# A two-layer decoder on one core: from a front half and a back half with their own buffers to two streams that each carry every other batch

## The chip, the cores and the metric

One Trainium2 chip, one core. The metric is the device time of one execution in microseconds (us). Four batches of 512 tokens by 256 channels pass through the decoder; nothing is sent to another core.

## The reference, cut to what matters

Each batch goes through six blocks, each of them "x = layernorm(x + block(x))":

```python
x = _layernorm(x + _L0_attn_ref(x, ...))                      # causal softmax attention, one head of 256
x = _layernorm(x + _L0_xattn_ref(x, ctx, ctx, mask, ...))     # masked cross attention, then its own layernorm
x = _layernorm(x + _L0_ffn_ref(x, k0, k1, k2, ...))           # +1/-1 weights, 512 -> 1024 -> 1024 -> 256
x = _layernorm(x + _L1_attn_ref(x, ...))                      # 16 heads, relu features, running sums
x = _layernorm(x + _L1_xattn_ref(x, ctx, ctx, ...))           # mLSTM: 8 heads, gates, decay matrix
x = _layernorm(x + _L1_ffn_ref(x, w1, conv_w, conv_b, w2))    # rounded linear, 3-tap convolution, silu, rounded linear
```

## The kernel before

The batch is cut into a **front half** (self attention "self", cross attention "cross", signed layers "sign", relu attention "perf") and a **back half** ("mlstm" and the rounded network "quant"). Tokens are in four tiles of 128. Each half has a set of buffers of its own (activations x and y, turned activations xT and ctxT, a work region, small columns) and four of the eight PSUM banks, which it uses in rotation. `front_half(b)` works in set 0 and `back_half(b)` in set 1, so the front of batch b+1 runs beside the back of batch b. That gives five stages: the front of batch 0 alone (stage 0), three stages with a front and a back side by side (stages 1 to 3), and the back of batch 3 alone (stage 4).

Each of the halves is a generator for each engine, which yields the name of a step before it issues the step's instructions. `weave` (L344) merges the generators of an engine: it always takes the step with the lowest due time. The due times are the tables `FRONT_TIMES` and `BACK_TIMES` (L40, L169), one column for each engine, plus 189 for each batch; the back of batch b starts with the front of b+1. The order so found is the order of the instructions in the queue of the engine, and each engine works its queue strictly from the front. Stage 0 also carries "prep" steps (`PREP_TIMES`, L293): ScalarE (ACT) makes the signed weights (`prep.w1*`, `prep.w2`, L2057 and L2060) and sums absolute values (`prep.abs*`, L2068), VectorE (DVE) rounds the weights of the last network (`prep.round*`, L1515 to L1520).

The lines that matter below:

- L824 `keep_clock(u, n)`: n matmuls of 512 bf16 columns (L827) into a bank that is free, whose result nobody reads. It stands ahead of the last product of the self attention of batch 0 (8) and of its `sign.xT0` (7), in every front half ahead of `perf.ft` (2, twice), `perf.state` (3, twice), `perf.fq.1` and `perf.fk.1` (3 each), in every back half ahead of `mlstm.cols` (3, in the last 6), and in the last back half ahead of `mlstm.xT0` (8), `quant.turn0` (8), `quant.row1` (6) and `quant.topT` (8). That makes 115.
- `perf` on TensorE (PE): feature products L1063 and L1077, states L1097, scores L1115. `mlstm.cols` begins at L1258; `mlstm.head*` follow.
- `quant`: DVE writes the hidden tile (L1954) and adds two of the three taps (L1966, L1969) to the middle one, which ACT makes (L2274). In the last back half PE makes two taps with diagonal matrices (`two_taps`, L1362; the matrices are built on POOL at L2391), DVE adds the third (L1962) and ACT skips its tap.
- `quant.down`: four token tiles of eight matmuls (L1409), each matmul behind the rounding of its slice of the hidden layer. In the last back half the first three tiles are made together, slice by slice (L1399).
- `front_half` on PE waits, ahead of the first self score (L872), for ACT's copies of both q and v.
- ctxT is loaded twice a batch, once for each half.

Of the kernel before, what the change touches and what calls it, by code (L numbers as in the profile page):

```python
# [8 lines left out]
U8 = mybir.dt.uint8  # L9
# [23 lines left out]
AMONG = ("cv0", "cv1")  # L33

FRONT_TIMES = [  # L40
    ("self.q", 1, None, 1, None),
    ("self.v", 2, None, 2, None),
    ("self.score0", 3, 4, 3, None),
    ("self.cv0", 4, 5, None, None),
    ("self.score1", 5, 6, 4, None),
    ("self.cv1", 6, 7, None, None),
    ("self.score2", 7, 9, 5, None),
    ("self.product0", 8, 10, 8, None),
    ("self.score3", 9, 11, 9, None),
    ("self.stats0", None, 13, None, None),  # L50
    ("self.product1", 10, 12, 10, None),
    ("self.score4", 11, 14, 11, None),
    ("self.product2", 12, 15, 12, None),
    ("self.norm0", None, 16, 13, None),
    ("self.stats1", None, 19, None, None),
    ("self.score5", 13, 17, 14, None),
    ("self.product3", 14, 18, 15, None),
    ("cross.shift0", None, 21, None, None),
    ("cross.shift1", None, 23, None, None),
    ("self.norm1", None, 20, 17, None),  # L60
    ("cross.shift2", None, 24, None, None),
    ("cross.xT0", 16, None, 16, None),
    ("cross.shift3", None, 25, None, None),
    ("cross.fold", 15, None, 19, None),
    ("cross.bar0", None, 26, None, None),
    ("cross.bar1", None, 27, None, None),
    ("cross.bar2", None, 28, None, None),
    ("self.rstd0", None, None, None, 4),
    ("cross.q0", 19, None, 20, None),
    ("cross.bar3", None, 30, None, None),  # L70
    ("cross.xT1", 20, 31, None, None),
    ("cross.score0", 23, 33, 23, None),
    ("self.rstd1", None, None, None, 5),
    ("cross.score1", 24, 34, 24, None),
    ("cross.q1", 22, None, 22, 6),
    ("cross.score2", 25, 37, 28, None),
    ("cross.product0", 26, 41, 29, None),
    ("cross.score3", 28, 42, 30, None),
    ("cross.in_stats0", None, 44, None, None),
    ("cross.product1", 29, 43, 31, None),  # L80
    ("cross.in_norm0", None, 45, None, None),
    ("cross.score4", 30, 46, 32, None),
    ("cross.product2", 31, 47, 34, None),
    ("cross.add0", None, 49, None, None),
    ("cross.in_rstd0", None, None, None, 7),
    ("cross.stats0", None, 50, None, None),
    ("cross.score5", 32, 51, 36, None),
    ("cross.product3", 33, 52, 37, None),
    ("cross.in_stats1", None, 53, None, None),
    ("cross.in_norm1", None, 54, None, None),  # L90
    ("cross.add1", None, 56, None, None),
    ("cross.rstd0", None, None, None, 8),
    ("cross.stats1", None, 57, None, None),
    ("cross.norm0", None, 55, 39, None),
    ("cross.in_rstd1", None, None, None, 9),
    ("sign.xT0", 38, 66, 44, None),
    ("sign.early", 47, None, None, None),
    ("cross.norm1", None, 67, 49, None),
    ("sign.xT1", 48, 70, 50, None),
    ("sign.a0", 52, 76, 51, None),  # L100
    ("cross.rstd1", None, None, None, 11),
    ("sign.a1", 53, 77, 52, None),
    ("sign.a2", 57, 78, 53, None),
    ("sign.a3", 58, 79, 54, None),
    ("sign.a4", 59, 80, 56, None),
    ("sign.a5", 60, 83, 57, None),
    ("sign.a6", 61, 84, 58, None),
    ("sign.a7", 62, 85, 60, None),
    ("sign.b0", 64, 86, 61, None),
    ("sign.b1", 65, 94, 63, None),  # L110
    ("sign.b2", 66, 97, 66, None),
    ("sign.b3", 67, 98, 67, None),
    ("sign.b4", 68, 102, 68, None),
    ("sign.b5", 69, 103, 69, None),
    ("sign.b6", 70, 108, 70, None),
    ("sign.c0", 72, 110, None, None),
    ("sign.b7", 71, 109, 71, None),
    ("sign.c1", 73, 111, None, None),
    ("sign.c2", 74, 113, None, None),
    ("sign.stats0", None, 112, None, None),  # L120
    ("sign.c3", 75, 115, None, None),
    ("sign.norm0", None, 114, 73, None),
    ("sign.stats1", None, 116, None, None),
    ("sign.norm1", None, 117, 75, None),
    ("perf.v0", 78, 119, None, None),
    ("perf.xT1", 79, 120, None, None),
    ("perf.qk.0", 80, 122, 76, None),
    ("perf.fq.0", 84, 129, 78, None),
    ("perf.q.1", 87, None, 80, None),
    ("perf.xT0", 77, None, 74, 22),  # L130
    ("perf.fk.0", 90, 133, 83, None),
    ("perf.k.1", 91, 134, None, None),
    ("perf.v1", 81, 124, None, 23),
    ("perf.ft.0", 93, 136, 86, None),
    ("perf.state.0", 94, 140, None, None),
    ("sign.rstd0", None, None, None, 20),
    ("perf.score0.0", 98, 143, 91, None),
    ("perf.before.0", 99, None, None, None),
    ("perf.score1.0", 100, 145, 94, None),
    ("sign.rstd1", None, None, None, 21),  # L140
    ("perf.den0.0", 101, None, None, None),
    ("perf.score2.0", 103, 150, 96, None),
    ("perf.num0.0", 102, None, None, None),
    ("perf.inverse.0", None, 153, None, None),
    ("perf.score3.0", 104, 152, 99, None),
    ("perf.den1.0", 105, None, None, None),
    ("perf.spread.0", 107, 155, 100, None),
    ("perf.num1.0", 106, None, None, None),
    ("perf.fq.1", 108, 159, 103, None),
    ("perf.fk.1", 109, 162, 106, None),  # L150
    ("perf.ft.1", 110, 164, 107, None),
    ("perf.state.1", 112, 166, None, None),
    ("perf.score0.1", 114, 169, 108, None),
    ("perf.vpad.0", None, None, None, 24),
    ("perf.before.1", 115, None, None, None),
    ("perf.score1.1", 116, 171, 111, None),
    ("perf.den0.1", 117, None, None, None),
    ("perf.num0.1", 118, None, None, None),
    ("perf.vpad.1", None, None, None, 25),
    ("perf.score2.1", 119, 175, 116, None),  # L160
    ("perf.den1.1", 121, None, None, None),
    ("perf.score3.1", 120, 177, 117, None),
    ("perf.inverse.1", None, 180, None, None),
    ("perf.num1.1", 122, None, None, None),
    ("perf.spread.1", 125, 184, 120, None),
    ("perf.out0", 128, 190, None, None),
    ("perf.out1", 129, 191, None, None),
]
BACK_TIMES = [  # L169
    ("first.stats0", None, 1, None, None),  # L170
    ("first.stats1", None, 3, None, None),
    ("first.norm0", None, 2, 6, None),
    ("first.rstd0", None, None, None, 1),
    ("first.norm1", None, 8, 7, None),
    ("first.rstd1", None, None, None, 2),
    ("mlstm.xT1", 18, 22, None, None),
    ("mlstm.xT0", 17, None, 18, 3),
    ("mlstm.gate", None, 29, None, None),
    ("mlstm.logf", None, 32, None, None),
    ("mlstm.softplus", None, None, 21, None),  # L180
    ("mlstm.csum", None, 35, None, None),
    ("mlstm.raw0", 21, None, 25, None),
    ("mlstm.g", None, 36, None, None),
    ("mlstm.high", None, 38, None, None),
    ("mlstm.nmd", None, 39, None, None),
    ("mlstm.part2", None, 40, None, None),
    ("mlstm.negated", None, None, 26, None),
    ("mlstm.part1", None, None, 27, None),
    ("mlstm.raw1", 27, None, 33, None),
    ("mlstm.cols", 34, None, None, None),  # L190
    ("mlstm.part3", None, 48, 35, None),
    ("mlstm.head0", 35, 58, 40, None),
    ("mlstm.head1", 36, 59, 41, None),
    ("mlstm.head2", 37, 60, 42, None),
    ("mlstm.state1", 40, 62, None, None),
    ("mlstm.head3", 39, 61, 43, None),
    ("mlstm.state2", 43, 65, None, None),
    ("mlstm.head4", 41, 63, 45, None),
    ("mlstm.weigh", None, None, 38, 10),
    ("mlstm.head5", 42, 64, 46, None),  # L200
    ("mlstm.head6", 44, 68, 47, None),
    ("mlstm.state3", 46, 71, None, None),
    ("mlstm.head7", 45, 69, 48, None),
    ("mlstm.ratio0", None, 72, None, None),
    ("mlstm.out0", 49, None, None, None),
    ("mlstm.ratio1", None, 74, None, None),
    ("mlstm.before1", 50, None, None, None),
    ("mlstm.out1", 51, None, None, None),
    ("mlstm.square0", None, 73, 55, None),
    ("mlstm.before2", 54, None, None, None),  # L210
    ("mlstm.var0", None, 81, None, None),
    ("mlstm.out2", 55, None, None, None),
# [2340 lines left out]
```

## Time and profile before

| | |
|---|---|
| median of 3 runs | 880.99 us (879.77 to 881.17) |
| span of the profiled execution | 877.1 us, 3.9 us under the median |
| PE busy | 765.2 us, 87% |
| DVE busy | 585.4 us, 67% |
| ACT busy | 360.3 us, 41% |
| POOL busy | 149.1 us, 17% |
| DMA queues busy | 8.7% of the 16 engines |
| mean granted TensorE clock | 0.963 of full speed |

Full speed of the clock is 2.4 GHz; the other level that appears is 0.50, 1.2 GHz. "Idle before, releaser" in a row is the time in which the engine waited in front of the instruction and what ended it. Rows of a timeline give start, duration, engine, line, operation and count. The profiled execution has a time of its own only as the span; what lies around it is the difference to the median.

### The profile page before, as it was taken

How to read it: one execution, taken by the hardware profiler on the slowest of the kernel's cores; microseconds unless marked ns; L12 is line 12 of the kernel's file. 1: busy time of each engine (PE TensorE's matmuls, PEld its weight loads, DVE VectorE, ACT ScalarE, POOL GpSimd, SP SyncE). 2: the span in 40 equal slices, each digit the busy share in tenths (PEclk: the TensorE clock that was granted, in tenths of full speed). 3: DMA queues.
4: the chain of work that ended last, by engine and by line, in shares of the span. 5: the costliest groups of instructions: out<-in, count | busy, mean ns of one | idle time of the engine just before them, and what ended most of it. 6: DMA issues, size and time to landing. Idle time of an engine off the chain costs nothing.

```text
span 877.1 us, 14966 instructions
## 1 busy us (share of the span) xinstructions
PE 765.2 (87%) x5976; PEld 517.8 (59%) x6028; DVE 585.4 (67%) x1478; ACT 360.3 (41%) x649; POOL 149.1 (17%) x228
## 2 busy tenths in 40 slices
PE   8897987788999988899999997999999998767394
PEld 5664455566685546676675555766774655646132
DVE  1645643335795778766886678856966697856676
ACT  2473122213643246534642166335632275362052
POOL 4011020000151220011142210012413200024200
PEclk9998999999999999999999999999999999988596
DMA  9420000010010000020010000020010000000000
GB/s 349 167 73 0 1 1 25 1 46 28 25 50 1 1 3 24 2 96 1 25 49 1 1 25 2 2 72 1 1 49 1 0 3 1 26 1 1 0 0 25
DMA packets 13525, 25.88 MB, mean 30 GB/s; under 512 B 784, under 2 KB 7056, under 8 KB 13200
## 3 DMA queue, kind: packets, MB, share of 16 engines
q1 hardware_dynamic: 13456, 24.92, 8.2%
q8 instruction: 48, 0.79, 0.4%
q14 instruction: 21, 0.17, 0.1%
HBM read 22.82 MB, written 2.10 MB: 28 GB/s over the span
## 4 chain that ended last, share of the span: by engine, by line
PE 35%; DVE 10%; ACT 2%; issue 2%; POOL 1%; DVEq 0%; ACTq 0%
PE bank L1020 6%; PE bank L841 3%; PE bank L1115 2%; PE bank L849 2%; PE bank L1323 2%; PE bank L1362 2%; PE bank L1030 2%; PE bank L1008 1%; DVE work L1827 1%; PE bank L1097 1%; PE bank L827 1%; PE bank L872 1%; DVE stats L1448 1%; PE bank L1330 1%; PE bank L892 1%
## 5 line engine op out<-in xcount | busy, mean ns | idle before, releaser
L2334 POOL TENSOR_TENSOR rstd<-rstd,minus_half 128x2 f32<-128x2 f32 x56 | 41.8, 746 | 443.7 <-DVE rstd L1454 443.7
L1020 PE MATMUL bank<-work,f0w 128*128 128x512 f16 x512 | 111.2, 379 | 0.0
L1020 PEld LDWEIGHTS bank<-work,f0w 128*128 128x128 f16 x512 | 50.1, 98 | 59.7
L2162 ACT ACTIVATE work<-bank 128x512 f16<-128x512 f32 x64 | 37.5, 596 | 98.7 <-PE bank L1020 73.0
L1663 DVE SCALAR_TENSOR_TENSOR work<-bank,work 128x512 f16<-128x512 f32 x64 | 42.5, 687 | 28.1 <-ACT work L2162 28.0
L827 PE MATMUL bank<-bar_upper,identb 128*128 128x512 bf16 x107 | 32.3, 419 | 21.5 <-DVE x L1463 8.4
L1531 DVE TENSOR_REDUCE small<-bank 128x1 f32<-128x512 f32 (+3 forms) x32 | 18.8, 588 | 48.0 <-PE bank L873 39.9
L892 PE MATMUL bank<-work 128*128 128x256 f32 x208 | 49.2, 380 | 1.0 <-ACT work L2091 1.0
L2200 ACT ACTIVATE work<-bank 128x512 f32<-128x512 f32 x32 | 19.1, 596 | 66.3 <-PE bank L1115 66.3
L2413 POOL TENSOR_TENSOR small<-small,minus_half 128x8 f32<-128x8 f32 x16 | 26.2, 1640 | 96.4 <-DVE small L1886 96.4
L1115 PE MATMUL bank<-work 64*128 64x128 f32 x512 | 38.1, 289 | 5.1 <-issue 4.0
L892 PEld LDWEIGHTS bank<-work 128*128 128x128 f32 x208 | 37.6, 190 | 5.7 <-ACT work L2091 1.5
L1744 DVE TENSOR_TENSOR work<-bank,upper 128x512 f32<-128x512 f32 x32 | 22.0, 689 | 24.3 <-PE bank L1115 24.3
L1448 DVE BATCH_NORM_STATS2 stats<-y 128x6 f32<-128x256 f32 x96 | 36.0, 414 | 1.7 <-ACT y L2140 1.7
L1115 PEld LDWEIGHTS bank<-work 64*128 64x128 f32 x512 | 31.9, 191 | 7.8 <-issue 7.1
L841 PE MATMUL bank<-xT,perf_w 128*128 128x512 f32 x64 | 30.4, 607 | 6.3 <-ACT work L2187 3.2
L2077 ACT ACTIVATE work<-bank,small 128x512 f32<-128x512 f32 (+3 forms) x32 | 19.4, 606 | 37.1 <-DVE small L1531 26.7
L827 PEld LDWEIGHTS bank<-bar_upper,identb 128*128 128x128 bf16 x124 | 11.4, 105 | 39.1 <-ACT work L2187 12.1
L2048 ACT ACTIVATE x<-y,shift,rstd 128x256 f32<-128x256 f32 x20 | 11.9, 597 | 49.4 <-DVE shift L1460 49.4
L1827 DVE TENSOR_TENSOR work<-work 128x512 f32<-128x512 f32 x32 | 28.2, 923 | 4.5 <-ACT work L2254 4.4
L1323 PEld LDWEIGHTS bank<-work 128*128 128x128 f32 x256 | 30.1, 192 | 1.9 <-issue 1.5
L1323 PE MATMUL bank<-work 128*128 128x66 f32 (+1 forms) x256 | 30.2, 271 | 0.9 <-DVE work L1827 0.8
(291 smaller groups left out, 1775.6 us busy)
## 6 DMA issues: line engine op xcount, KB each, us to landing
ctxT<-in_ctxT SPq DMA_DIRECT2D x8, 512.0 KB, 4.7
work<-in_mask SPq DMA_DIRECT2D x4, 1024.0 KB, 5.5
xT<-in_xT SPq DMA_DIRECT2D x4, 512.0 KB, 3.6
work<-in_w SPq DMA_DIRECT2D x1, 2048.0 KB, 18.6
ctx<-in_ctx SPq DMA_DIRECT2D x4, 512.0 KB, 3.9
perf_w<-in_perf_w SPq DMA_DIRECT2D x1, 1536.0 KB, 15.8
out<-y SPq DMA_DIRECT2D x3, 512.0 KB, 3.0
x<-in_x SPq DMA_DIRECT2D x2, 512.0 KB, 7.7
```

What stands on the lines that cost most here:

```text
L827: nc.tensor.matmul(u.bank[:, :], identb[:, :], bar_upper[:, :, :].rearrange("p a b -> p (a b)"), start=True, stop=True)
L841: ins = nc.tensor.matmul(u.bank[:, :], weights[:, k, c0:c0 + P], src[:, k, :], start=(k == 0), stop=(k == NC - 1))
L892: ins = nc.tensor.matmul(u.bank[:, 0:C], probT[:, t % 2, j * P:(j + 1) * P], v[:, j, :], start=(j == 0), stop=(j == n - 1))
L1020: ins = nc.tensor.matmul(u.bank[:, :], f0w1[:, k, m * P:(m + 1) * P], h1[part][:, k, :], start=(k == 0 and part == 0), stop=(k == NF - 1 a ...
L1115: ins = nc.tensor.matmul(u.bank[:, here], kf[rows, pair, here], qf[rows, pair, here], start=(i == 0), stop=True, tile_position=(PM * i, 0) ...
L1323: ins = nc.tensor.matmul(u.bank[:, h * LV1:(h + more) * LV1], cT[:, h, t * P:(t + 1) * P], values_[:, h * LV1:(h + more) * LV1], start=Tru ...
L1448: m = vec.mark(nc.vector.bn_stats(s.stats[:, t, :], src[:, t, :]))
L1663: low_part(what, m, dst, number + m, lambda o, x, hi: nc.vector.scalar_tensor_tensor(out=o, in0=x, scalar=0.0, in1=hi, op0=ALU.max, op1=AL ...
L1827: nc.vector.tensor_tensor(cT[:, h, :], cT[:, h, :], decay[h % 2], ALU.mult).then_inc(decayed.sem, 1)
L2162: nc.scalar.activation(dst[0][:, m, :], u.bank[:, :], ACT.Relu).then_inc(high_made.sem, 1)
L2334: nc.gpsimd.tensor_tensor(s.rstd[:, two], s.rstd[:, two], minus_half[:, 0:2], ALU.pow).then_inc(s.rstd_made.sem, 1)
L2413: nc.gpsimd.tensor_tensor(var[:, g], var[:, g], minus_half[:, 0:LH], ALU.pow).then_inc(group_rstd.sem, 1)
```

## The change

The two sets no longer belong to a half. There are two **streams**, each with a full set of buffers and four banks. Stream a takes batches 0 and 2, stream b batches 1 and 3, each front half and back half one after the other. The due times are gone; an explicit list of turns says how many steps of which stream each engine takes. Step for step these lists give the order of before in stages 1 to 4, but for one DVE step: the second `perf.out` addition stands ahead of the first statistics of the back half, not behind them. In stage 0 some prep steps have other places.

```diff
-def front_starts(b):
-    return b * PERIOD
-def back_starts(b):
-    return (b + 1) * PERIOD
+STREAMS = 2
+ROUNDS = B // STREAMS
+TURNS = {
...
+    "scalar":
+        "a11 p2 a2 p3 a7 p4 a4 p8 a49 b6 a2 b11 a2 b1 a1 b3 a3 b7 a1 b1 a1 b2 a1 b1 a4 b1 a4 b6 a1 b3 a1 b2 a1 b1 a2 "
...
+    "gpsimd":
+        "a16 b6 a1 b1 a8 b6 a2 b3 a6 b1 a1 b8 a6 b2 a3 b6 a1 b1 a8 b6 a2 b14",
+    "sync":
+        "w1 a1 w1 a1 w2 a1 w1 a1 w2 b4 w1 a4 b1 a3 b6 a2 b2",
+}
...
+        def whole(s):
+            for n in range(ROUNDS):
+                yield from front_half(s, n)
+                yield from back_half(s, n)
+        weave({"a": whole(first), "b": whole(second), "p": prep()}, TURNS["scalar"])
```

What the last stage and the single halves lose:

```diff
-        def keep_clock(u, n, later=True):
-            pe.wait_ge(*(u.free if later else u.read))
-            for _ in range(n):
-                nc.tensor.matmul(u.bank[:, :], identb[:, :], bar_upper[:, :, :].rearrange("p a b -> p (a b)"), start=True, stop=True)
...
-                if b == B - 1 and j > 0:
-                    two_taps(j - 1)
...
-            early = 0 if b < B - 1 else NT - 1
...
-            for what in ("q", "v"):
-                for k in range(NC):
-                    pe.wait_ge(*fb["self", b, what, k].read)
+            def self_ready():
+                for k in range(NC):
+                    pe.wait_ge(*s.banks["self", n, "q", k].read)
```

All 115 matmuls of `keep_clock` go, and with them the two taps on PE, the matrices on POOL and the slice-by-slice `down`: the last batch is computed as the others are. The wait for v moves from ahead of the first self score to ahead of the first product. Stage 0, in the order of the queues:

```text
ACT before  ... cross.q0  w15 w16 w17 w2  cross.q1 score0 score1  abs x8  score2(+turn1) product0 score3 ...
ACT after   ... cross.q0 cross.q1  w15 w16 w17 w2  score0 score1 score2 turn1  abs x8  product0 score3 ...
DVE before  ... stats1 sign.xT0 ... sign.a5 prep.mean ... sign.b3  round x8  sign.b4 sign.b5 ...
DVE after   ... stats1 prep.mean sign.xT0 ... sign.b4  round x8  sign.b5 ...
PE before   ... product3 prep.sums sign.xT0 sign.early ...
PE after    ... product3 sign.xT0 prep.sums sign.early ...
```

Loads: ctxT comes once a batch; the raw signs stand in the place of the relu attention's weights, which are loaded behind the casts of the signs; the raw weights of the last network stand in the two context tiles, so the context tiles are loaded behind the rounding. In the second round mask, x, xT, ctxT and context of a stream are loaded behind the steps of its first batch that read the places last. The first self product of the second round waits for the stream's store. POOL clears six tiles at the start where it cleared three.

## Rows read from the trace of the kernel before

**Rows 1.** Busy time of each engine by stage; columns: stretch, length, busy (count), clock, DMA
```profile
0.00:191.70 191.70, 162.39 (x1175) 105.08 (x1187) 84.74 (x232) 61.40 (x118) 22.74 (x41) 0.96 0.19 71
191.70:382.20 190.50, 177.04 (x1466) 122.61 (x1477) 141.22 (x354) 84.70 (x155) 33.93 (x50) 1.00 0.07 21
382.20:572.80 190.60, 177.05 (x1466) 122.58 (x1477) 142.73 (x357) 86.24 (x157) 33.93 (x50) 1.00 0.07 23
572.80:763.70 190.90, 177.89 (x1466) 123.38 (x1477) 142.05 (x357) 86.45 (x157) 33.86 (x50) 0.99 0.05 15
763.70:877.10 113.40, 70.81 (x408) 44.19 (x412) 74.65 (x179) 41.49 (x65) 24.68 (x37) 0.79 0.03 10
```

**Rows 2.** The filler matmuls, all of line L827: min/median/max ns, first and last start
```profile
L827 PE MATMUL bank<-bar_upper,identb x107: 377/379/634, 30.1 to 853.8; 128*128 128x512 bf16 x107
```

**Rows 3.** Timeline of PE in stage 1: what follows two filler groups of the relu attention
```profile
350.38 1.14 PE L1063 MATMUL bank<-work,perf_w 32*128 32x512 f32 x8 [0.75 <-DVE y L1758]
...
355.88 0.95 PE L1077 MATMUL bank<-perf_w,work 32*128 32x128 f32 x24 [0.22 <-DVE work L1712]
```

**Rows 4.** Three stretches of 3.4 us with their clock; columns as in rows 1
```profile
170.60:174.00 3.40, 3.24 (x33) 2.53 (x37) 1.68 (x9) 0.55 (x1) 0.00 (x0) 0.50 0.00 0
...
351.50:354.90 3.40, 1.98 (x14) 0.55 (x11) 3.19 (x6) 3.32 (x8) 0.00 (x0) 1.00 0.00 0
...
628.00:631.40 3.40, 3.07 (x16) 2.18 (x17) 3.02 (x11) 1.36 (x3) 2.65 (x5) 0.50 0.00 0
```

**Rows 5.** Timeline of PE: first masked scores of the second head group, batches 0 and 1
```profile
171.30 2.08 PE L1115 MATMUL bank<-work 64*128 64x128 f32 x16
...
361.98 1.16 PE L1115 MATMUL bank<-work 64*128 64x128 f32 x16
```

**Rows 6.** Timeline of PE: start of the gate columns and of sign.b0, stages 2 and 3
```profile
435.04 0.44 PE L1258 MATMUL bank<-small,ones 8*128 8x72 f32 x2
...
463.33 1.03 PE L1020 MATMUL bank<-work,f0w 128*128 128x512 f16 x4
...
625.58 0.44 PE L1258 MATMUL bank<-small,ones 8*128 8x72 f32 x2
...
654.09 1.24 PE L1020 MATMUL bank<-work,f0w 128*128 128x512 f16 x5
```

**Rows 7.** Timeline of stage 0: PE's cross.q1, then ACT's casts, exponentials and absolute sums
```profile
46.73 1.03 PE L971 MATMUL bank<-xT,cross_w 128*128 128x256 f32 x4
...
45.31 3.49 ACT L2057 ACTIVATE f0w<-ctxT,signed 128x1024 f16<-128x1024 uint8 x3
48.70 2.18 ACT L2060 ACTIVATE f0w<-y 128x512 f16<-128x512 uint8 x4
...
51.50 0.68 ACT L2077 ACTIVATE work<-bank,small 128x512 f32<-128x512 f32 x1
...
53.32 0.62 ACT L2068 ACTIVATE f1w<-work 128x512 bf16<-128x512 f32 x1
...
60.03 0.69 ACT L2077 ACTIVATE work<-bank,small 128x512 f32<-128x512 f32 x1 [0.21 <-DVE small L1535]
```

**Rows 8.** Timeline of DVE in stage 0: first and last instruction of the rounding
```profile
97.73 0.48 DVE L1515 TENSOR_SCALAR work<-work,s_sum 128x512 f32<-128x512 f32 x1
...
108.28 0.23 DVE L1523 TENSOR_TENSOR wgT<-wgT 128x80 f32<-128x80 f32 x1
```

**Rows 9.** Timeline of PE in stage 2: the first self score
```profile
390.03 0.68 PE L872 MATMUL bank<-xT,work 128*128 128x128 f32 x4 [0.77 <-ACT work L2106]
```

**Rows 10.** DVE groups by form: one tap in the last stage, two taps in stage 3
```profile
L1962 DVE SCALAR_TENSOR_TENSOR work<-work,columns,bank 128x512 f32<-128x512 f32 x8 | 6.0, 747 | 4.8 <-PE bank L1362 4.3
...
L1969 DVE SCALAR_TENSOR_TENSOR work<-work,columns 128x512 f32<-128x512 f32 x8 | 6.1, 756 | 0.3
...
L1966 DVE SCALAR_TENSOR_TENSOR work<-work,columns 128x512 f32<-128x512 f32 x8 | 5.9, 732 | 0.0
```

**Rows 11.** Timeline of PE in the last stage: the last token tile of quant.down
```profile
868.53 1.91 PE L1409 MATMUL bank<-f1w,work 128*128 128x256 bf16 x8
```

More of the change, by code:

```diff
@@ L33 @@
 AMONG = ("cv0", "cv1")
[L40 to L168, printed above, removed]
@@ new lines, with weave @@
+ROUNDS = B // STREAMS
+TURNS = {
+    "tensor":
[4 rows of a table added]
+    "vector":
[7 rows of a table added]
+    "scalar":
[5 rows of a table added]
+    "gpsimd":
[3 more added lines that the diff above has]
+}
+def weave(programs, turns):
+    ahead = {name: next(program, None) for name, program in programs.items()}
+    for turn in turns.split():
+        name = turn[0]
+        for _ in range(int(turn[1:])):
+            assert ahead[name] is not None, name
+            ahead[name] = next(programs[name], None)
+    assert not any(ahead.values()), ahead
@@ L700, in build @@
-    k1u = [a[:, :, :].rearrange("p a b -> p (a b)").bitcast(U8).rearrange("p (k n) -> p k n", k=NF // 2)
-           for a in (back.xT, back.ctxT)]
-    k2u = back.y[:, :, :].rearrange("p a b -> p (a b)")[:, 0:NF * C // 4].bitcast(U8).rearrange("p (k n) -> p k n", k=NF)
-    w1, w2 = w.cut(NC, FH), w.cut(NF, C)
-    absum = w.cut(8)
-    fold_w = w.cut(2, NC, C)
-    fb, bb = front.banks, back.banks
-    def plan_prep():
-        bb.use(("prep", "abs"))
-    def plan_attention(name, b, among=()):
+    first, second = streams
@@ L796, in build @@
-    plan_prep()
-    fb.use("fold")
-    for b in range(B):
-        plan_front(b)
-        plan_back(b)
+                s.banks.use(("mlstm", n, "before", t))
+            s.banks.use(("mlstm", n, "out", t))
+        s.banks.use(("quant", n, "turn", 0))
+        s.banks.use(("quant", n, "row1"))
+        s.banks.use(("quant", n, "turn", 1))
+        for j in range(NF):
+            s.banks.use(("quant", n, "hidden", j))
+        s.banks.use(("quant", n, "topT"))
+        s.banks.use(("quant", n, "row2"))
@@ L802, in build @@
+        for t in range(NT):
+            s.banks.use(("quant", n, "down", t))
+    first.banks.use("fold")
+    for each in streams:
+        for n in range(ROUNDS):
+            plan_front(each, n)
+            plan_back(each, n)
     tiled = "b (t p) c -> b p t c"
@@ L977, in front_half, with cross_ready @@
[L977 removed]
+            def cross_ready():
+                pe.wait_ge(*s.bar2_made.all(n))
+            yield from attention(s, "cross", n, s.ctxT, s.c_v, lambda t: s.bar2[:, t, :], False, cross_ready)
             yield "sign.xT0"
[L980 to L983 removed]
+            wait_normed(s, n, 2, 0)
@@ L1228, in raw_scores @@
             def raw_scores(k):
-                four = [bb["mlstm", b, "raw", k * LHT + i] for i in range(LHT)]
+                four = [s.banks["mlstm", n, "raw", k * LHT + i] for i in range(LHT)]
                 for u in four:
@@ L1605, in spread_by_gamma @@
+            cross_read = [s.banks["cross", n, "product", t].read for t in range(NT)]
             def spread_by_gamma(p):
@@ L1717, in front_half @@
                 yield f"perf.state.{c}"
-                u = fb["perf", b, c, "state"]
+                u = s.banks["perf", n, c, "state"]
+                if n == 0 and s is second:
+                    dve.wait_ge(*rounded_w.at(0))
                 dve.wait_ge(*u.full)
@@ L2491, in build @@
+        weave({"a": whole(first), "b": whole(second), "w": weights()}, TURNS["sync"])
+        for each in streams:
+            sp.wait_ge(each.stored.sem, 16 * (ROUNDS + 1))
     sync_engine()
```

1750 lines of the change are left out of this document (764 added, 986 removed), and 15 rows, old and new, of the table TURNS.

## Prediction

> **What bounds the kernel now.** I read the stages first. In stages 1 to 3 TensorE is busy for 177 of 190.6 us, with VectorE at 142 behind it; in stage 0 it is busy for 162 of 191.7 us and in stage 4 for 71 of 113.4, where short chains over all engines set the pace [rows 1]. So PE's queue sets the time, plus the 13.5 us a paired stage, 29 us in stage 0 and 43 us in stage 4 in which it waits for a result. The instruction order is the second thing: the lists of turns give nearly the order that the trace shows, so the pipeline is not new. Five stages stay five stages. What is left is what was taken out, three places in stage 0, and the waits at stage borders. Times are summed against the profiled span of 877.1 us; the median of the runs is 880.99, 3.9 more, and I add that at the end. A measurement of this kernel can tell about 0.2% (1.8 us) from no change.
>
> **The fillers.** 115 matmuls whose result nobody reads go [rows 2]. What they cost where they stand is read from what follows. Behind the group at the start of the second head group, PE still waits 0.75 us for DVE; behind that ahead of the third product, 0.22 us [rows 3]. The instruction behind a group is released by ACT or DVE, so the group lay in time that was idle anyway. I count their removal as nothing, but for the three in front of the gate columns in stages 1 to 3, where PE has no wait: 0.3 us a stage. At the most they cost 0.24 us each, 28 us in all; at the least nothing.
>
> Their cover was the clock. The clock is full almost throughout stages 1 to 3 and 0.79 in stage 4 [rows 1]. It was granted at 0.50 at 170.6, just after a stretch of small state products, and at 628.0, after the gate columns, although three fillers stood there [rows 4]. Without fillers more of such places fall to 1.2 GHz. At 351.5 PE is busy for only 1.98 of 3.4 us, six fillers among it [rows 4].
>
> What one such stretch costs has two prices. Sixteen score matmuls took 2.08 us at the low clock and 1.16 at the full one: 0.92 us for one group [rows 5]. From the gate columns to sign.b0 it is 28.29 us in stage 2 and 28.51 in stage 3, which had the low stretch: 0.22 us, as the heads there wait for DVE [rows 6]. The ends are 0.2 us and half of a 3.4 us stretch, 1.7 us. The relu attention is a chain in which PE's time is on the path, so I take 1.2 us there, and three stretches (from the first state, the second key features, the second state): +3.6 us a stage, between 0.6 and 5.1. For stage 0 +4.0. In the gate columns I take 0.2, inside the 0.3 above.
> The Trainium skill, TensorE: Matmul & The Clock Gate, in its Terms, prices throttled time at half its length, 1.7 us a stretch; the pair in rows 6 shows 0.22, so the trace disagrees where PE is not the last to arrive. By that rule the three paired stages would lose 5.1 us each instead of 3.6.
>
> **Stage 0, the order on ACT.** PE's cross.q1 is done at 47.76. ACT had used the wait for it to make casts from 45.31 on; after them came cross.q1's copy and the first exponential at 51.50 [rows 7]. Now q1 comes first (two copies, done about 48.6), and the casts (3.49 + 2.18, less overlap 5.6 us) stand ahead of the exponential: it starts at about 54.2, +2.7 us. PE has made scores 0 and 1 by 51.5 and waits there for 3.5 us, so the clock should fall and score 2 run at half pace: +1.6. The eight absolute sums (0.62 each, 5.0 us) began at 53.32, beside PE's score 2, and held only score 2's exponential, by 2.3 us; now they stand behind it and ahead of product 0 and of score 3's exponential, which was at 60.03 [rows 7]. It moves to about 66.9: exponential 2 at 60.3, copy, sums, product, then it. That is +6.8 us on the path of product 3, the norms and sign.xT0; 5.2 without the clock. The mean of the weights (0.5 us on DVE) moves ahead of sign.xT0: +0.5. The order of the self attention's turns frees a copy early, but the casts on DVE hold the next step: 0.
>
> **Stage 0, the rounding.** It takes DVE from 97.73 to 108.51 and had stood behind sign.b3 [rows 8]. It now begins one tile later, when DVE has read b4, near 100.7, and ends at 111.5; b5, b6 and b7 are read until 113.4, and PE's first c tile needs them. It could otherwise end at 112.07: +1.6 us.
>
> **The border waits.** Ahead of the first self score PE waited 0.77 us for ACT's copy of v [rows 9], 0.98 in stage 0. The q copies were done long before: -0.8 in each of stages 1 to 3, -1.0 in stage 0. The second `perf.out` addition ahead of the statistics costs DVE 0.7 us in stage 4 (in the others the back half's first PE step is 20 us off); what it no longer waits for, ACT's last norm of the batch before, gives 0.4 back: +0.3.
>
> **Stage 4.** Without the eight fillers ahead of mlstm.xT0 the turned values and gates run at the low clock: +1.6; the six ahead of the gate columns had held these by 1.4 us: together with the +0.3, and slower first heads, +1.0. At quant the token turn and hidden 0 are at 1.2 GHz: +0.7. The taps: the loop took 20.7 us, 2.3 us a tile, paced by PE with taps. Now DVE makes hidden, two taps and a maximum. A tap was 0.75 us with PE's two taps as input, and two taps are 0.73 + 0.76 [rows 10]; with overlap a tile is 2.8 us of DVE, but the maxima that stood idle now fill in: 21.7 us, +1.0 (between 0 and 2.5). ACT's tap (0.8 us) goes beside DVE. The turned maxima +0.3. `down`: four tiles one after the other behind the last rounding at 867.5 instead of one; a tile at the low clock takes 1.7 to 1.9 us [rows 11]. Statistics 0 starts 0.7 later, tile 3 ends near 872.8, against a DVE that read it at 871.65: +1.0 (0 to 2.0). POOL's matrices went beside a wait: 0. Sum +4.0.
>
> **What else moves.** Half of ctxT's loads go; DMA is idle but at the start, where the order of the loads that the first stage needs is the same: 0. The loads of the second round wait for steps that end before those of before did, or in the same place; the store waits for nothing that is queued behind it on SP, and the first self product comes 14 us after its stage's start: 0. Three more tile clears on POOL (under 1 us each) end before the first score at 16.4: 0. Banks rotate over the same four users within a half: 0.
>
> **Sum.** Stage 0: -1.0 + 6.8 + 0.5 + 1.6 + 4.0 = +11.9. Stages 1 to 3: 3 x (-0.8 - 0.3 + 3.6) = +7.5. Stage 4: +4.0. Together +23.4: 900.5 in the span, 904.4 in the measurement.
>
> **The rivals.**
> *The clock does not fall further.* The fillers were more than was wanted, as in stages 1 to 3 only one stretch was low. For it: many of the places are followed by large matmuls. Against: at 628.0 even three fillers did not do. Then 1.6, 4.0, 3 x 3.6 and some 2 in stage 4 go: 886.
> *The fillers were on the path (the faster side).* Behind several groups the wait is only 0.2 us, and if the results that PE waits for are themselves made later because of fillers ahead, their time returns. The place is the relu attention and the gate columns of stages 0 to 3. Against: the releasers are ACT and DVE, which follow PE's products and not the fillers. Half of them would give 14 us; with no clock falling, 886 - 14 = 872. It decides once more than 21 of the 115 (0.24 us each, for the 5 us of the other changes) come back without the clock being lost.
> *The clock stays low through the relu attention.* Stage by stage, small matmuls at the low clock, PE as part of the chain, five to six stretches instead of three: +3 more a stage and +4 in stages 0 and 4: 920.
> *The change does not do what it says:* that the turns of stage 0 cost little, as PE finds other work. It has none in its queue. With the clock kept too it would be 881.
>
> **How the numbers follow.** Forecast 0.68 (its own range 895 to 914), the clock kept 0.14, low throughout 0.08, fillers on the path 0.06, nothing much 0.04. The range must leave out no more than 2 in 10: from the rival at 886, with its spread a little under it, to the high one cut: 887 to 918. Faster by over 0.2%: 0.07; within 0.2%: 0.03; slower: 0.90.
>
> **What would show it.** Right: stage 0 longer by about 12 us, of which 7 lie between cross.q1 and sign.xT0, with ACT's casts ahead of the first exponential and PE idle there; the c tiles of stage 0 waiting for DVE; more slices of the clock under full speed in the relu attention of every stage; no L827; a conv loop of 21 to 22 us; stages 1 to 3 at 192 to 194 us. Wrong: stages 1 to 3 under 190 us (fillers were on the path), a mean clock as high as before (the first rival), or new idle time of PE at a stage border with a load or a store as releaser.

## The result, and the profile after

The changed kernel takes **925.3 us** (median of 4 executions, 919.97 to 928.55) where the kernel before, on the same chip, takes 880.4 (879.64 to 881.17): 1.051 times as long, 95% interval 1.046 to 1.056. The forecast was 904.4 with a range to 918: right in sign, and 21 us too small; the rise was forecast at 23.4 us and is 44.9. These few executions spread by 0.9%, those of before by 0.2%. The profiled one took 928.55 us, with a span of 927.3.

Two statements ahead of this section are wrong, and are put right here. `keep_clock` issued **124** matmuls, not 115: the sum left out the nine ahead of the gate columns in stages 1 to 3 (the bound of 28 us for all of them becomes 30). And the slice-by-slice `quant.down` did not go: L1048 of the changed kernel reads `early = 0 if n < ROUNDS - 1 else NT - 1`, and the last round of a stream is batch 2 in stream a and batch 3 in stream b. So the last stage keeps it and stage 3 gets it as well.

The stages of the changed kernel, by the start of their first self product and the end of the last `perf.out`; columns as in [rows 1]:

```profile
0.00:213.30 213.30, 173.05 (x1155) 114.75 (x1156) 83.99 (x229) 61.16 (x118) 24.84 (x44) 0.87 0.18 66
213.30:411.50 198.20, 184.50 (x1460) 128.96 (x1459) 142.26 (x357) 84.77 (x155) 34.41 (x50) 0.93 0.06 18
411.50:609.90 198.40, 183.21 (x1460) 128.64 (x1459) 142.97 (x358) 86.09 (x157) 34.14 (x50) 0.95 0.06 20
609.90:809.40 199.50, 183.41 (x1459) 128.52 (x1457) 143.17 (x358) 86.23 (x157) 34.16 (x50) 0.95 0.02 6
809.40:927.30 117.90, 51.37 (x344) 38.33 (x344) 78.68 (x187) 46.71 (x73) 20.14 (x29) 0.67 0.02 7
```

Against [rows 1], TensorE (PE) has fewer matmul records in stages 1 to 3 (1460 for 1466) and is busy for longer (in stage 1 184.5 us for 177.0). VectorE's (DVE's) and ScalarE's (ACT's) columns are as before in stages 0 to 3; in stage 4, where they now make all three taps, they are 4 and 5 us longer. The DMA column is no higher anywhere. The clock is the column that moved: 0.87, 0.93, 0.95, 0.95, 0.67 for 0.96, 1.00, 1.00, 0.99, 0.79.

| stage | before | after | more | predicted |
|---|---|---|---|---|
| 0 | 191.7 | 213.3 | 21.6 | 11.9 |
| 1 | 190.5 | 198.2 | 7.7 | 2.5 |
| 2 | 190.6 | 198.4 | 7.8 | 2.5 |
| 3 | 190.9 | 199.5 | 8.6 | 2.5 |
| 4 | 113.4 | 117.9 | 4.5 | 4.0 |

Where it sits inside stage 1 is read from PE's timeline, from the end of the first head group to the scores of the second:

```profile
369.63 1.13 PE L868 MATMUL bank<-work,head_spread 128*128 128x128 f32 x8 [0.62 <-DVE work L1418]
372.16 1.99 PE L749 MATMUL bank<-work,perf_w 32*128 32x512 f32 x8 [1.40 <-DVE y L1423]
376.03 2.09 PE L749 MATMUL bank<-work,perf_w 32*128 32x512 f32 x8 [1.89 <-ACT work L1843]
379.59 1.67 PE L762 MATMUL bank<-perf_w,work 32*128 32x128 f32 x24 [1.46 <-DVE work L1375]
381.18 1.11 PE L1041 MATMUL bank<-ident,work 128*128 128x128 f32 x4
382.45 5.31 PE L781 MATMUL bank<-work 128*128 128x68 f32 x24 [0.15 <-DVE work L1371]
387.56 2.05 PE L1007 MATMUL bank<-ident,small 128*128 128x128 f32 x8
...
389.97 2.08 PE L799 MATMUL bank<-work 64*128 64x128 f32 x16
...
408.04 3.62 PE L532 MATMUL bank<-perf_w,y 128*128 128x256 f32 x16
```

The same place in the kernel before: the `spread` product, the state and `perf.out`.

```profile
347.85 1.13 PE L1184 MATMUL bank<-work,head_spread 128*128 128x128 f32 x8 [0.62 <-DVE work L1753]
...
358.03 2.84 PE L1097 MATMUL bank<-work 128*128 128x68 f32 x24
...
378.76 3.62 PE L849 MATMUL bank<-perf_w,y 128*128 128x256 f32 x16
```

Before, the first feature product took 1.14 us and the third product 0.95 [rows 3], the scores 1.16 [rows 5]; now it is 1.99, 1.67 and 2.08. The longest single item is the state, 24 products of 68 columns: 5.31 us for 2.84. The waits in brackets are those that the fillers had covered: 1.40, 1.89 and 1.46 us, each still ended by DVE or ACT. Both halves of the story are in these lines: the fillers did stand in idle time, and what stood behind them now runs at half pace. The clock of the same place, in stretches of 3.4 us:

```profile
371.20:374.60 3.40, 1.99 (x8) 0.42 (x8) 3.04 (x5) 2.44 (x5) 0.00 (x0) 0.66 0.00 0
374.60:378.00 3.40, 1.97 (x8) 0.55 (x8) 1.65 (x3) 2.32 (x5) 0.00 (x0) 0.50 0.00 0
378.00:381.40 3.40, 1.94 (x29) 1.62 (x26) 2.01 (x4) 1.25 (x3) 0.00 (x0) 0.50 0.00 0
381.40:384.80 3.40, 3.25 (x15) 2.88 (x15) 2.12 (x6) 0.71 (x2) 0.00 (x0) 0.50 0.00 0
384.80:388.20 3.40, 3.40 (x18) 3.40 (x18) 0.41 (x1) 0.00 (x0) 0.00 (x0) 0.50 0.00 0
388.20:391.60 3.40, 3.40 (x22) 2.78 (x23) 2.52 (x10) 0.00 (x0) 0.00 (x0) 0.50 0.00 0
391.60:395.00 3.40, 3.40 (x65) 2.70 (x63) 1.62 (x3) 1.64 (x3) 0.00 (x0) 0.82 0.02 5
```

The low level lasts here for 20.5 us without a break (a stretch at 0.66 is low for 0.68 of it, one at 0.82 for 0.36), and this part of stage 1 is 7.5 us longer: from the `spread` product (369.63) to `perf.out` (408.04) 38.41 us, before 30.91. Slices of 3.4 us over the other stages give, in the relu attention of stages 2 and 3, 6.8 us at the low level around the first state and 13.6 at the second head group, and in that of stage 0 10.2 and 20.5.

Stage 0 on ACT, which answers to [rows 7]: cross.q1's copies, the seven casts, the first exponential, the third one, the first of the eight absolute sums, and the fourth exponential behind them.

```profile
48.18 0.84 ACT L1789 ACTIVATE work<-bank,columns 128x256 f32<-128x256 f32 x2 [4.58 <-PE bank L660]
48.91 3.49 ACT L1713 ACTIVATE f0w<-perf_w,signed 128x1024 f16<-128x1024 uint8 x3
52.30 2.17 ACT L1716 ACTIVATE f0w<-work 128x512 f16<-128x512 uint8 x4
54.38 0.67 ACT L1732 ACTIVATE work<-bank,small 128x512 f32<-128x512 f32 x1
...
60.31 0.69 ACT L1732 ACTIVATE work<-bank,small 128x512 f32<-128x512 f32 x1 [4.50 <-DVE small L1195]
...
61.45 0.64 ACT L1723 ACTIVATE f1w<-ctx 128x512 bf16<-128x512 f32 x1
...
66.72 0.68 ACT L1732 ACTIVATE work<-bank,small 128x512 f32<-128x512 f32 x1
```

They stand at 54.38, 60.31 and 66.72; the prediction had 54.2, 60.3 and 66.9. The first signed product (`sign.early`) starts at 79.07 and not at 70.96. The near match in absolute time holds some luck: `cross.q0` began 1.9 us earlier than before (38.91 for 40.83), and `cross.q1` then ran at the low clock, 3.75 us for 1.97.

### The profile page after: what moved, and what is told of

It is laid out like the page before. It is cut to its first block and busy times, and to the rows that moved or that the text cites. A ratio compares the mean times of both kernels' runs of the same rounds, so it can differ in the third digit from the quotient of the medians.

```text
span 927.3 us, 14710 instructions
## 1 busy us (share of the span) xinstructions
PE 775.5 (84%) x5872; PEld 539.2 (58%) x5872; DVE 591.1 (64%) x1486; ACT 365.0 (39%) x657; POOL 147.7 (16%) x223
## 5 line engine op out<-in xcount | busy, mean ns | idle before, releaser
L781 PE MATMUL bank<-work 128*128 128x68 f32 x192 | 39.3, 395 | 6.9 <-DVE work L1371 6.9
L781 PEld LDWEIGHTS bank<-work 128*128 128x128 f32 x192 | 38.3, 308 | 8.9 <-ACT work L1839 7.3
L799 PE MATMUL bank<-work 64*128 64x128 f32 x512 | 41.7, 308 | 0.0
L577 PEld LDWEIGHTS bank<-work 128*128 128x128 f32 x208 | 38.8, 196 | 4.6
L799 PEld LDWEIGHTS bank<-work 64*128 64x128 f32 x512 | 35.1, 209 | 9.4 <-issue 8.7
L749 PE MATMUL bank<-work,perf_w 32*128 32x512 f32 x128 | 21.5, 742 | 15.0 <-ACT work L1843 7.6
L556 PE MATMUL bank<-ctxT,work 128*128 128x512 f32 x64 | 31.5, 617 | 0.0
L1000 PEld LDWEIGHTS bank<-work 128*128 128x128 f32 x256 | 30.1, 192 | 1.3 <-issue 0.9
```

The source lines that it names most:

```text
L577: ins = nc.tensor.matmul(u.bank[:, 0:C], s.probT[:, t % 2, j * P:(j + 1) * P], v[:, j, :], start=(j == 0), stop=(j == tiles - 1))
L781: ins = nc.tensor.matmul(u.bank[:, o:o + more * PV1], s.kfs[:, t - 1, j * P:(j + 1) * P], values_[:, t - 1, h * PV1:(h + more) * PV1], sta ...
L799: ins = nc.tensor.matmul(u.bank[:, here], s.kf[rows, pair, here], s.qf[rows, pair, here], start=(i == 0), stop=True, tile_position=(PM * i ...
L1000: ins = nc.tensor.matmul(u.bank[:, h * LV1:(h + more) * LV1], s.cT[:, h, t * P:(t + 1) * P], values_[:, h * LV1:(h + more) * LV1], start=T ...
```

## Experiments

All times are medians, each beside runs of the kernel before on the same chip: 880.0 us for the first four kernels, 878.3 for the next four, 878.6 for the last four. The first four ran on another chip than the rest, so a difference between two groups holds up to 1.7 us of the chip. Beside the experiments, with 13 to 22 executions, the kernel before spreads by 1.1 to 1.2%.

| kernel | us | against before, 95% |
|---|---|---|
| changed, relu fillers back | 889.9 | 1.012 (1.006 to 1.018) |
| changed, ACT's old order | 916.1 | 1.041 (1.036 to 1.047) |
| before, no fillers | 914.8 | 1.041 (1.034 to 1.047) |
| changed, everything back | 876.3 | 0.996 (0.994 to 0.999) |
| changed, feature fillers only | 921.2, once 897.9 | none given |
| changed, the other ten only | 904.9 | 1.029 (1.023 to 1.036) |
| before, fillers of 16 columns | 912.3 | 1.038 (1.032 to 1.044) |
| everything back, more fillers | 874.6 | 0.995 (0.992 to 0.998) |
| everything back, old wait for v | 877.5 | 0.997 (0.994 to 1.000) |
| changed, old orders | 913.6 | 1.038 (1.033 to 1.043) |
| old orders and relu fillers | 880.5 | 1.000 (0.998 to 1.003) |
| most fillers | 870.9 | 0.989 (0.985 to 0.993) |

**1. The fillers of the relu attention back in the changed kernel.**

```diff
+                    if c > 0:
+                        keep_clock(four[0], 3)      # fq.1, fk.1
...
+                keep_clock(four[0], 2)              # ft.0, ft.1
...
+                keep_clock(u, 3)                    # state.0, state.1
```

> The changed kernel with the 16 filler matmuls of the relu attention put back in every front half (3 each ahead of the second head group's query and key features, 2 ahead of each third product, 3 ahead of each state). Theory A (the lost clock in the relu attention is nearly the whole excess over the prediction): that section, which grew by about 9 us a stage in four stages, returns to its old length, 925.3 - 36 = about 889 us, and the mean clock rises above 0.94. Rival B (the two buffer sets themselves, with later loads and other waits, cost part of it): the sections recover only the 3.6 to 4.0 us of the prediction, 910 us.

889.9 us: 35.4 of the 44.9 us come back, with 64 matmuls that compute nothing. Theory A gave 889. The mean clock of the profiled execution is 0.938 for 0.892, just short of the 0.94 that was expected.

**2. ACT's order of stage 0 back.**

```diff
-        "a11 p2 a2 p3 a7 p4 a4 p8 a49 ...
+        "a11 p2 a2 p3 a6 p4 a3 p8 a51 ...
```

> The changed kernel with ScalarE's stage 0 in the order of before (four weight casts ahead of cross.q1's copy, the eight absolute sums ahead of the third cross exponential), no fillers. The prediction counted 6.8 us for this order, the traces show sign.early 8.1 us later. Theory A: 6.5 to 7.5 us come back, 918 us. Rival C (PE's idle time there is lost because the clock is low or for another reason, not by ACT's order): under 2 us, 924 us.

916.1 us, 9.2 less, where 6.5 to 7.5 were expected. In its trace `sign.early` starts at 68.96 and not at 79.07; 1 us of these 10 is an earlier start of the whole, and 1.8 are `cross.q1`, which stands on PE ahead of the place where the two orders part. First the changed kernel, then this one:

```profile
44.39 3.75 PE L660 MATMUL bank<-xT,cross_w 128*128 128x256 f32 x8 [0.87 <-DVE xT L1102]
```

```profile
43.45 1.97 PE L665 MATMUL bank<-xT,cross_w 128*128 128x256 f32 x8 [0.88 <-DVE xT L1107]
```

The traces of experiments 5 and 6 have the changed order and 1.97 us there, so these 1.8 us are the clock of the single execution and not the order. Behind them the order costs 7.4 us in this pair of traces (7.6 and 5.9 with the traces of experiments 5 and 6 in the place of the first).

**3. The kernel before, without its fillers.**

```diff
             pe.wait_ge(*(u.free if later else u.read))
-            for _ in range(n):
-                nc.tensor.matmul(u.bank[:, :], identb[:, :], ...)
```

> The kernel before, everything as it was, with all 115 filler matmuls left out (their waits stay). Theory A: it loses what the changed kernel lost by them: 44.9 of the whole, less about 7 for stage 0's order, the taps and the border waits, so +38 us, 918 us, mean clock near 0.90. Rival B: the fillers are worth the 15 to 18 us of the prediction and the rest belongs to the two buffer sets, 897 us. Rival D (fillers were on the path): faster than 880.

914.8 us. The old buffers, the old lists and the old waits lose 34.7 us by this alone, so that much of the loss doesn't belong to the two streams. The hypothesis that fillers were on the path falls with it.

**4. Everything back in the changed kernel.** The fillers in all their places, the two taps on PE with their matrices from POOL, the orders of ACT and DVE in stage 0, and batch 2's `down` tile by tile; the streams, their loads and the place of the wait for v stay as changed.

> The changed kernel with everything that came along taken back: all 115 fillers, the two taps on PE in the last batch, before's order of ScalarE and VectorE in stage 0, and batch 2's down products tile by tile. What is left of the change are the two buffer sets, the loads and the border waits. Theory A: 880.4 less 3 us for the wait for v: 877 us. Rival B: the sets cost something themselves, 885 us or more.

876.3 us, with an interval below 1. Two full buffer sets cost nothing that can be measured, and this version is a little faster than the kernel before. Its timeline beside that of experiment 1 also shows the price of the slice-by-slice `down` in stage 3. First experiment 1, then this one; the rows run from the `down` tiles to `perf.out`:

```profile
764.38 2.79 PE L1067 MATMUL bank<-f1w,work 128*128 128x256 bf16 x24
767.01 1.06 PE L877 MATMUL bank<-work,head_spread 128*128 128x128 f32 x8
767.90 1.04 PE L1077 MATMUL bank<-f1w,work 128*128 128x256 bf16 x8
769.74 0.48 PE L537 MATMUL bank<-perf_w,y 128*128 128x256 f32 x1 [0.80 <-DVE y L1432]
```

```profile
748.39 1.92 PE L1116 MATMUL bank<-f1w,work 128*128 128x256 bf16 x16
750.15 1.06 PE L889 MATMUL bank<-work,head_spread 128*128 128x128 f32 x8
751.05 1.91 PE L1116 MATMUL bank<-f1w,work 128*128 128x256 bf16 x16
752.79 1.46 PE L545 MATMUL bank<-perf_w,y 128*128 128x256 f32 x6
```

Twenty-four products ahead of the spread instead of 16 delay it by 0.87 us; the eight behind it no longer cover DVE's work on its result, and PE waits for 0.80. From the first row of each to `perf.out` it is 5.36 us for 4.40. So stage 3 pays about 1 us for a rearrangement that only the last stage can use.

**5 and 6. Which of the sixteen a half.** One kernel has only the six at the features of the second head group, the other only the ten at the third products and the states.

> The changed kernel with six fillers a front half, those ahead of the second head group's query and key features alone. Theory A (a filler keeps a clock that is still up, and the long low stretch begins exactly there): the 5.4 to 7.5 us a stage behind these features come back, the 3.3 to 4.4 us of the first state in stages 0, 2 and 3 stay: 925.3 - 26 = 899 us. Rival E (fillers help in proportion to their number, 6 of 16): 925.3 - 0.375 x 35.4 = 912 us.

> The changed kernel with the other ten fillers of the relu attention, 2 ahead of each third product and 3 ahead of each state, none at the second head group's features. Theory A: the first state's 3.3 to 4.4 us in stages 0, 2 and 3 come back, while the clock has already fallen when the second third product is reached and ten narrow gaps don't bring it up: 925.3 - 11 = 914 us. Rival E (in proportion, 10 of 16): 903 us.

With the six, three of four executions took 921.2 us, which neither theory gave, and one took 897.9, which is theory A's 899. With the ten it is 904.9, rival E's 903 and not theory A's 914. The profile of the six is of one of the three longer executions. PE in stage 1 with the six features' fillers, from the second of them on:

```profile
370.70 0.82 PE L515 MATMUL bank<-bar_upper,identb 128*128 128x512 bf16 x3 [0.73 <-ACT work L1850]
371.73 1.14 PE L756 MATMUL bank<-work,perf_w 32*128 32x512 f32 x8 [0.20 <-ACT work L1850]
374.33 0.95 PE L769 MATMUL bank<-perf_w,work 32*128 32x128 f32 x24 [1.47 <-DVE work L1382]
...
376.48 5.30 PE L788 MATMUL bank<-work 128*128 128x68 f32 x24 [0.61 <-DVE work L1378]
...
384.00 2.08 PE L806 MATMUL bank<-work 64*128 64x128 f32 x16
```

The features keep their clock (1.14 and 0.95 us), and it falls just ahead of the state, which then takes 5.30 us. With the ten it is the other way:

```profile
361.80 1.14 PE L754 MATMUL bank<-work,perf_w 32*128 32x512 f32 x8 [1.40 <-DVE y L1430]
364.85 2.09 PE L754 MATMUL bank<-work,perf_w 32*128 32x512 f32 x8 [1.91 <-ACT work L1850]
367.57 1.04 PE L515 MATMUL bank<-bar_upper,identb 128*128 128x512 bf16 x2 [0.64 <-ACT work L1850]
368.54 1.67 PE L768 MATMUL bank<-perf_w,work 32*128 32x128 f32 x24
370.14 1.11 PE L1048 MATMUL bank<-ident,work 128*128 128x128 f32 x4
371.04 1.49 PE L515 MATMUL bank<-bar_upper,identb 128*128 128x512 bf16 x3
372.32 3.60 PE L788 MATMUL bank<-work 128*128 128x68 f32 x24
375.75 1.14 PE L1014 MATMUL bank<-ident,small 128*128 128x128 f32 x8
```

The clock falls at the features and is back within the state (3.60 us, the next group 1.14). In slices of 3.4 us both traces have 10.2 us at the low level in this place, for the 20.5 of the changed kernel, and from the `spread` product to `perf.out` it is 35.7 us with the six and 34.6 with the ten, for 38.4 with none and 30.9 with all sixteen (experiment 1). So each part cuts the low stretch by half, at another end of it, and only both together bring all of it back. Which part is worth more in the whole time, and what decides whether the six give 897.9 or 921.2, stays open.

**7. The kernel before with narrow fillers:** the second operand `identb[:, 0:16]`, so 16 columns instead of 512.

> The kernel before with all 115 fillers in place, each of 16 columns and not of 512: the same waits and the same number of instructions in PE's queue, almost no work. Theory A (what the fillers do is work that holds the clock): as without any, 914.75 us, clock 0.91. Rival F (they act by their place in the queue, by holding back PE's other instructions or keeping it awake): 880 us.

912.3 us, as without any. The trace has all of them:

```profile
L827 PE MATMUL bank<-identb x124: 169/173/221, 29.7 to 886.2; 128*128 128x16 bf16 x124
```

With the same waits and instructions in the same places of PE's queue the kernel is as slow as without any: the 2.4 us to experiment 3 are inside the intervals (1.032 to 1.044 and 1.034 to 1.047). What brings the 35 us is the work in the wide ones.

**8. More fillers in the last stage.**

```diff
             yield "mlstm.raw1"
+            if is_last(s, n):
+                keep_clock(first.banks["quant", n, "down", NT - 1], 16, False)
             raw_scores(1)
...
+                keep_clock(u, 6)                    # ahead of the second token row
...
+                keep_clock(first.banks["taps", NF - 1], 9, False)
```

> The version with everything taken back, plus fillers in idle time of the last stage: 16 ahead of the second half of the raw scores (4.33 us idle there), 12 instead of 8 ahead of the turned maxima, 6 ahead of the second token row and 9 behind it. Theory A (in the last stage too the clock is what the small products cost): raw scores 2.09 -> 1.17, gate columns and the six fillers 5.7 -> 3.5, token row 2.08 -> 1.0, last down tile 1.91 -> 1.0: about 4 us less than the version with everything back, 872 us. Rival G (DVE and ACT set the last stage's end, the fillers delay what stands behind them): 876 us or more.

874.6 us for 876.3: the size is smaller than expected, and the intervals of the two overlap. Inside the profile the last stage, from `perf.out` on, is 114.8 us for 117.8.

**9. The border waits.** Experiment 4 with the wait for v ahead of the first self score again.

> The version with everything taken back, but with the wait for v ahead of the first self score, as before, not ahead of the first product. What is left of the change are the buffer sets and the loads alone. Theory A (the 3.7 us by which that version beats the kernel before are the four border waits, 0.8 to 1.0 us each): 880 us, no difference from before. Rival H (the gain comes from the loads or the buffers): 876 us.

877.5 us, 1.2 more than experiment 4 and between the theories. The trace shows the wait as predicted, 0.77 us at the border to stage 2 (in [rows 9] it was 0.77 as well), and the score 7.82 us behind the stage's first product for 6.89 without it:

```profile
387.66 0.68 PE L569 MATMUL bank<-xT,work 128*128 128x128 f32 x4 [0.77 <-ACT work L1819]
```

The four waits are 3.3 us (three of 0.77, one of 0.98 in stage 0), the medians differ by 1.2, and the single executions of each kernel spread by 7. So the size of this term in the whole time, and whether the buffers and loads bring anything of their own, stay open. They cost nothing: the ratio to the kernel before is not above 1.

**10. Before's orders, no fillers.** ACT as in 2, DVE's mean and rounding at their old places, `down` tile by tile for batch 2.

> The changed kernel without any filler or taps, with before's orders in stage 0 (ScalarE and VectorE: the mean and the rounding in their old places) and with batch 2's down tile by tile. It is the kernel before without fillers (914.75) less the border waits (3.6) plus the last stage's missing taps (1 to 2): theory A 912 to 913 us. Against the run with ScalarE's order alone (916.1) the rounding gives back 2.1 and the down 0.8 us: 913. Rival (these small terms hide behind the clock's losses): 916 us.

913.6 us, 2.5 less than experiment 2, where 2.9 were expected. The intervals of the two overlap and they ran on different chips, so the medians agree with the expectation but don't show these small terms.

**11. The same with the sixteen fillers a half.**

> As the version with everything back (876.3), but with the fillers of the relu attention alone: none in stage 0's first blocks, ahead of the gate columns or in the last stage, and no taps on PE. Theory A: the last stage loses 3 us (taps 1 to 2, the start of the gates 1.3), stage 0 1 us, the gate columns nothing: 880 us. Rival: the gate columns' fillers carry something too, as a low stretch there goes on into the heads: 884 us.

880.5 us, 33.1 less than experiment 10. To experiment 4 there are 4.3 us, and they lie in the last stage: from `perf.out1` on 120.1 us for 116.1. Stages 1 and 2 take 189.7 and 190.8 us in this one and 189.8 and 190.0 in that, so the three fillers ahead of the gate columns there carry nothing that can be told from the traces.

**12. Most fillers.** Experiment 8, and in stage 0 14 instead of 7 ahead of `sign.xT0` and 5 ahead of `sign.early`.

> The version with more fillers in the last stage, and in stage 0 14 instead of 7 ahead of the third block's first turned tile and 5 more ahead of its first products, where PE idles 1.85 and 1.48 us and where the clock was 0.50 in two of three profiles (the block's first 32 products 7.63 us instead of 4.5). Theory A: 1 to 2 us less than 874.6, 873 us, a spread smaller than before's. Rival G: no difference, 875 us.

870.9 us, the fastest, 1.1% under the kernel before (0.985 to 0.993); the six executions spread by 0.5%. The interval overlaps that of experiment 8 (0.992 to 0.998). In stage 0 the groups fill what was idle, and the products behind them run in 1.49 us, where they took 2.72 in experiment 8:

```profile
65.67 3.18 PE L523 MATMUL bank<-bar_upper,identb 128*128 128x512 bf16 x14
...
71.32 1.49 PE L701 MATMUL bank<-work,f0w 128*128 128x256 f16 x12 [0.29 <-DVE work L1366]
```

But in the trace of experiment 4, with only seven fillers there, they took 1.47 us, so one trace of each doesn't show that the added ones did it. Stage 0 as a whole is 179.3 us here, 182.6 in experiment 8 and 178.5 in experiment 4.

In the last stage the second half of the raw scores takes 1.17 us, here and in experiment 8, where it took 2.09 in the kernel before, in the changed one and in experiment 4:

```profile
773.12 3.63 PE L523 MATMUL bank<-bar_upper,identb 128*128 128x512 bf16 x16
777.51 1.17 PE L943 MATMUL bank<-xT,ctxT 32*128 32x128 f32 x32 [0.77 <-ACT work L1948]
```

## Why the prediction was wrong in size and right in sign

The kernels, put one behind the other, share out the difference: 925.3, less 9.2 (ACT's order), less 2.5 (rounding, mean, batch 2's down), less 33.1 (relu fillers), less 4.3 (the fillers and taps of the last stage), is 876.3. The last term also holds the 15 fillers of stage 0's first blocks and the nine ahead of the gate columns. The 33.1 is clear of the noise and the 9.2 nearly so (no execution of one lies among those of the other, but the intervals just touch); the 2.5 and the 4.3 are differences across two chips and no larger than the intervals are wide.

- **The clock in the relu attention: the step that failed.** The prediction took three low stretches of 3.4 us a stage at 1.2 us each: 3 x 3.6 and 4.0 for stage 0, 14.8 us over stages 0 to 3. The runs give 33.1 (experiments 10 and 11); in their traces it is 13.3, 8.6, 4.9 and 7.0 us in stages 0 to 3. The price was right: 20.5 us of low clock cost 7.5 in stage 1, which is 1.24 us for 3.4. The count was wrong: the changed kernel has six stretches in the relu attention of each of stages 1 to 3 and nine in that of stage 0, and these 27 at 1.2 us are 32.4 us. The prediction asked where the clock would fall, and took for granted that it comes back with the next busy stretch. It didn't: in the slices from 384.80 and 388.20 PE is busy for all of 3.4 us and the clock stays at 0.50. What runs there are the state products, the `L1007` group and the first scores; what about them leaves the clock down isn't shown. [Rows 4] had said so: at 170.6 the clock was 0.50 with PE busy for 3.24 of 3.40 us. That row was used as an example of where a fall happens, and not as one of how long it lasts. The row at 351.5 was misread too: three of its matmuls are fillers (0.82 us), not six. The sign that was named for being right, stages 1 to 3 at 192 to 194 us, didn't come: they took 198.2 to 199.5.
- The rival **"the clock stays low through the relu attention"** had the right mechanism, with its five to six stretches and its 920. It got 0.08. Its shares were off: it had 3 us more than the forecast in each of stages 1 to 3 and 4 in each of stages 0 and 4, and the table has 5.2, 5.3, 6.1, 9.7 and 0.5, so that its total lies near is in part luck. The Trainium skill (TensorE: Matmul & The Clock Gate, Terms) prices throttled time at half its length. By the mean clocks of the profiled executions, experiments 10 and 11 have 190 and 103 us at the low level; half of the difference is 43 us, and the runs show 33. So about three quarters of what its rule gives is found over these stages, and [rows 6] had shown a place where little of it is.
- **Fillers cost nothing where they stood:** nothing speaks against it. Putting them back (experiments 1, 11) and adding 47 to the 124 (experiment 12) never made a kernel measurably slower.
- **ACT's order in stage 0:** the times of the exponentials were right to 0.2 us, with the luck named above; the cost was 9.2 us by the medians of experiment 2, not 6.8. In the traces 1.8 us of it are `cross.q1` at the low clock, which isn't the order's doing; without them it is 7.4. Score 2 ran in 2.97 us for 1.88, 1.1 and not the 1.6 of the prediction. Behind PE's waits of 3.17 and 2.07 us the last sixteen products of the cross attention took 5.31 us, and 3.62 in experiment 2: 1.7 us that the prediction hadn't counted. With the mean (0.5) and the border wait (-1.0) `sign.early` should have come 6.3 us later and came 8.1 later.
- **The rounding one tile later:** predicted 1.6, in the traces 2.1 (`sign.c0` ends 9.9 us later than before, `sign.b0` began 7.8 later). It held DVE from 108.94 to 119.72, for the 10.8 us it had taken before.
- **The border waits:** -0.8 a stage and -1.0 in stage 0, shown in the trace of experiment 9; the medians show 1.2 us of these 3.3. The 0.3 a stage for the gate columns is too small for experiment 11 to tell.
- **Stage 4:** predicted +4.0, measured +4.5, in other shares. From `perf.out1` to the first head +2.2 (predicted 1.0); from there to the first hidden tile +0.3 (0.7); the loop to `down` +2.1 (1.3); `down` and the end 0.0 (1.0), as that part of the change was misread. The DVE loop was forecast well: 0.75 + 0.74 + 0.75 us a tile, 0.69 for the maximum, and 21.9 us from the first hidden tile to the last maximum (883.20 to 905.06) for a predicted 21.7 and 20.7 before. The rest of the 2.1 are 0.4 us ahead of this loop and 0.6 behind it, at the turned maxima (predicted 0.3).
- **The streams, the loads, the banks:** 0 predicted, and 0 or a small gain measured. Nothing in PE's waits has a load or a store as its releaser.

## What to carry to other kernels

Where a matmul's result is nobody's, ask what it does to the clock before it is taken out. Count the cost as the price of low time multiplied by how long the clock stays low, and don't take for granted that the next busy stretch ends it: here it lasted 20.5 us in one piece. A rewrite of the buffers or of the schedule should be measured with such small helpers kept: here the new structure cost nothing, and the things dropped on the way put 5% on top of it. The place for fillers here was time in which PE waited for another engine, and they acted by their work: 124 of 512 columns were worth 35 us, the same 124 with 16 columns nothing that could be measured.

## What was not expected

- A TensorE that its records show as busy from end to end can stay at the low clock: 10.2 us from 381.40 to 391.60, at 0.50 throughout, with 3.25 to 3.40 of each 3.4 us busy.
- The same six fillers were worth 4 us in three executions and 27 us in the fourth (experiment 5, 921.2 and 897.9 us). So a few executions of a kernel can mislead. The kernel before did as much: its spread was 0.2% in the four executions beside the changed kernel and 1.1 to 1.2% in the 13 to 22 beside the experiments, so that the 0.9% of the changed kernel is no sign of a less steady one.
- The 24 small products of the gate columns took 5.2 us in the last stage of the changed kernel (830.77 to 835.95) and 2.8 us in experiment 12, though they stream 8 rows and up to 72 columns each. So small products pay for the low clock as well.
